# Splitting the early second products of a mixture-of-experts kernel, with their preparation shared between GpSimd and ScalarE

## The reference, cut to what matters

```python
for e in range(E):                                   # 8 experts
    h = jax.nn.gelu(x_flat @ w1[e].T + b1[e], approximate=False)   # 128 -> 512
    y = h @ w2[e].T + b2[e]                                        # 512 -> 128
    out = out + comb[:, e:e + 1] * y
```

## Time and profile before

| | us |
|---|---|
| median of 3 runs (lowest, highest) | 190.15 (190.08, 190.45) |
| the profiled execution, device time | 190.0 |
| its span, first to last instruction | 188.1 |
| TensorE busy in the span | 176.1 (94%) |
| ScalarE, VectorE, GpSimd busy | 123.4, 117.9, 79.0 |

### The profile page before, as it was taken

How to read it: one execution, slowest core, us unless ns; L and a number is a source line. 1 busy time by engine, 2 the same in 40 slices (tenths; PEclk the granted TensorE clock), 3 DMA queues, 4 the chain that set the end, 5 groups by cost and what they waited for, 6 DMA issues and landing times.

```text
span 188.1 us, 3342 instructions
## 1 busy us (share of the span) xinstructions
PE 176.1 (94%) x1281; PEld 120.3 (64%) x1281; DVE 117.9 (63%) x199; ACT 123.4 (66%) x185; POOL 79.0 (42%) x68
## 2 busy tenths in 40 slices
PE   6999999879899998999989999799999999999991
PEld 3269767456467543447556557467787888878880
DVE  1569434858184388556065919878789686676673
ACT  3525834225737654344989498848878999999980
POOL 8304219973922084552436073505221243333312
PEclk9999999999999999999999999999999999999999
DMA  4997000000000000490000000000000590000001
GB/s 136 316 384 324 7 0 0 3 0 0 3 3 2 2 0 0 110 331 12 0 0 5 0 0 0 0 3 0 0 7 3 186 302 14 0 3 0 0 0 56
DMA packets 5647, 10.41 MB, mean 55 GB/s; under 512 B 1264, under 2 KB 1648, under 8 KB 5376
## 3 DMA queue, kind: packets, MB, share of 16 engines
q1 hardware_dynamic: 5216, 10.12, 15.5%
q10 hardware_dynamic: 416, 0.08, 0.2%
HBM read 9.65 MB, written 0.56 MB: 54 GB/s over the span
## 4 chain that ended last, share of the span: by engine, by line
PE 73%; issue 9%; DVE 7%; ACT 5%; POOL 4%; DVEq 0%; ACTq 0%; POOLq 0%
PE PS L1157 8%; PE PS L1161 7%; PE PS L1158 6%; PE PS L1187 6%; PE PS L1184 6%; PE PS L1185 5%; PE PS L1179 4%; POOL pairs L353 4%; PE PS L851 3%; PE PS L1029 2%; PE PS L1015 2%; PE PS L906 2%; PE PS L874 2%; PE PS L1102 2%; ACT room L513 2%
## 5 line engine op out<-in xcount | busy, mean ns | idle before, releaser
L513 ACT ACTIVATE room<-PS,b_sb 128x512 f32<-128x512 f32 x64 | 43.6, 688 | 23.9 <-PE PS L1161 22.5
L768 DVE TENSOR_TENSOR Gl<-room,Gh 128x512 fp32r<-128x512 f32 x50 | 41.2, 832 | 13.6 <-ACT Gh L458 13.0
L361 POOL TENSOR_TENSOR x_sb<-x_sb,room 128x512 f32<-128x512 f32 x15 | 23.5, 1566 | 57.6 <-DVE room L777 57.6
L1157 PE MATMUL PS<-x2h,w1h 128*128 128x512 f32 x64 | 27.4, 427 | 1.1 <-ACT room L513 0.6
L458 ACT ACTIVATE Gh<-room 128x512 fp32r<-128x512 f32 x40 | 25.3, 633 | 1.3
L1161 PE MATMUL PS<-x2l,w1h 128*128 128x512 f32 x64 | 25.5, 399 | 0.0
L1158 PE MATMUL PS<-x2h,w1l 128*128 128x512 f32 x64 | 25.2, 393 | 0.0
L1184 PE MATMUL PS<-Gh,w2h 128*128 128x512 f32 x50 | 20.9, 418 | 0.0
L1187 PE MATMUL PS<-Gl,w2h 128*128 128x512 f32 x50 | 19.8, 397 | 1.0 <-DVE Gl L768 1.0
L1185 PE MATMUL PS<-Gh,w2l 128*128 128x512 f32 x50 | 19.7, 395 | 0.0
L1157 PEld LDWEIGHTS PS<-x2h,w1h 128*128 128x128 f32 x64 | 12.0, 187 | 10.4 <-issue 4.9
(11 more groups left out here) (136 smaller groups left out, 292.6 us busy)
## 6 DMA issues: line engine op xcount, KB each, us to landing
room<-comb_rows SPq DMA_DIRECT2D x16, 256.0 KB, 6.0
w1raw<-w SPq DMA_DIRECT2D x8, 256.0 KB, 5.0
w_sb<-w SPq DMA_DIRECT2D x2, 1024.0 KB, 9.6
x_sb<-x SPq DMA_DIRECT2D x2, 256.0 KB, 3.2
out<-x_sb SPq DMA_DIRECT2D x2, 256.0 KB, 4.4
attw_sb<-attw SPq DMA_DIRECT2D x1, 320.0 KB, 5.4
cst<-consts SPq DMA_DIRECT2D x1, 228.5 KB, 5.1
convw_sb<-convw ACTq DMA_DIRECT2D x1, 80.0 KB, 3.2
```

Source lines behind the costliest of these rows:

```text
L361: nc.gpsimd.tensor_tensor(t2[:, cols(p)], t2[:, cols(p)], part[:, s, :], ALU.add).then_inc(acc_done, 1)
L513: nc.scalar.activation(G[:, n % GR, :], PS[:, U_BANK[n % 2], :], ACT.Gelu, bias=b1_sb[:, c:c + 1])\
L768: nc.vector.tensor_tensor(Gl[:, n % GR, :], G[:, n % GR, :], Gh[:, n % GR, :].bitcast(f32), ALU.subtract)\
L1157: mm(o, w1h[e][:, ms], x2h[:, cols(p)], start=True, stop=False)
```

## The change

All second products are split but those of steps 18 and 22 (before, steps 0 to 11, 17 and 18 were unsplit). For steps 0 to 11 ScalarE makes the casts, and GpSimd the differences of steps 0 to 9. In steps 0 to 10 second products lag by three steps (before, by one for steps 0 to 8). The w2 of experts 0 to 2 is cast ahead of the loop, behind the exponentials of the first images, and the others in steps 2 to 6. GpSimd's w2 differences are made ahead of rstd(3) for expert 0, and in steps 1, 3, 8, 10, 12, 17, 21 for the others.

```diff
-W2_ORDER = [3, 4, 5, 6, 7, 0, 1, 2]
+EARLY_W2 = 3
-        LAGS = [1] * 9 + [2, 3, 4, 2, 3, 4] + [5, 2, 3, 4] * 2 + [5, 2] + [3] * (MT * VISITS - 25)
+        LAGS = [3] * 11 + [4, 2, 3, 4] + [5, 2, 3, 4] * 2 + [5, 2] + [3] * (MT * VISITS - 25)
...
-        SPLIT0, ACT_HIGH = 3 * MT, 24
-        SPLIT = [n for n in range(SPLIT0, STEPS) if n not in (17, 18)]
-        HIGH_W2 = {n: e for n, e in enumerate(W2_ORDER)}
-        LOW_W2 = {n + 1: e for n, e in enumerate(W2_ORDER)}
+        DVE_HIGH = range(3 * MT, 24)
+        SPLIT = [n for n in range(STEPS) if n not in (18, 22)]
+        HIGH_W2 = {e - 1: e for e in range(EARLY_W2, E)}
+        LOW_W2 = {1: 1, 3: 2, 8: 3, 10: 4, 12: 5, 17: 6, 21: 7}
+        POOL_LOW = range(10)
+
+        def low_engine(n):
+            return "pool" if n in POOL_LOW else "dve"
...
+            def low_gelu(n):
+
+                pool.wait_ge(g_high[high_engine(n)], high_count(n))
+                nc.gpsimd.tensor_tensor(Gl[:, n % GR, :], G[:, n % GR, :], Gh[:, n % GR, :].bitcast(f32), ALU.subtract)\
+                    .then_inc(g_low["pool"], 1)
...
+            low_weights2(0)
             rstd(3)
             rstd(4)
...
                 if n in SCORES:
                     for s in range(2):
                         pair(SCORES[n], s)
+                if n in POOL_LOW:
+                    low_gelu(n)
                 if n in LOW_W2:
                     low_weights2(LOW_W2[n])
...
                 k = n - GR
                 if k in SPLIT:
-                    act.wait_ge(g_low, split_count(k))
+                    act.wait_ge(g_low[low_engine(k)], low_count(k))
...
+            for e in range(EARLY_W2):
+                high_weights2(e)
             norm_square(3)
...
-                if n >= ACT_HIGH:
+                if n in SPLIT and high_engine(n) == "act":
                     high_gelu(n)
...
-                if n in SPLIT and n < ACT_HIGH:
+                if n in SPLIT and high_engine(n) == "dve":
                     high_gelu(n)
-                if n in SPLIT:
+                if n in SPLIT and low_engine(n) == "dve":
                     low_gelu(n)
...
-                pe.wait_ge(g_low, split_count(n))
+                pe.wait_ge(g_low[low_engine(n)], low_count(n))
```

More of the change, by code:

```diff
@@ L181, in hybrid_program @@
         g_high = {name: sem(f"g_high_{name}") for name in ("act", "dve")}
-        g_low = sem("g_low")
+        g_low = {name: sem(f"g_low_{name}") for name in ("pool", "dve")}
         up_done, gelu_done, down_done = sem("up_done"), sem("gelu_done"), sem("down_done")
@@ L229, in hybrid_program, with low_count @@
         G_LOGITS, G_ORDER, G_EXP, G_WEIGHTS, G_ROWS = 0, 1, 2, 2, 4
-        SPLIT0, ACT_HIGH = 3 * MT, 24
-        SPLIT = [n for n in range(SPLIT0, STEPS) if n not in (17, 18)]
-        HIGH_W2 = {n: e for n, e in enumerate(W2_ORDER)}
-        LOW_W2 = {n + 1: e for n, e in enumerate(W2_ORDER)}
+        DVE_HIGH = range(3 * MT, 24)
[5 more added lines that the diff above has]
+            return "pool" if n in POOL_LOW else "dve"
+        def low_count(n):
+            return sum(low_engine(k) == low_engine(n) for k in SPLIT if k <= n)
         def high_engine(n):
-            return "dve" if n < ACT_HIGH else "act"
+            return "dve" if n in DVE_HIGH else "act"
         def high_count(n):
             return sum(high_engine(k) == high_engine(n) for k in SPLIT if k <= n)
-        def split_count(n):
-            return sum(k <= n for k in SPLIT)
         def downs(n):
@@ L338, in low_weights2 @@
             def low_weights2(e):
-                pool.wait_ge(w2h_ready, W2_ORDER.index(e) + 1)
-                if e == W2_ORDER[0]:
+                pool.wait_ge(w2h_ready, e + 1)
+                if e == 0:
                     pool.wait_ge(pv_done, 4)
@@ L456, in high_gelu @@
                 act.wait_ge(gelu_done, n + 1)
-                act.wait_ge(down_done, n - GR + 1)
+                if n == 0:
+                    act.wait_ge(pv_done, 4)
+                    act.wait_ge(sums_done, 4)
+                if n >= GR:
+                    act.wait_ge(down_done, n - GR + 1)
                 nc.scalar.activation(Gh[:, n % GR, :], G[:, n % GR, :], ACT.Copy)\
@@ L757, in high_gelu @@
                 dve.wait_ge(gelu_done, n + 1)
[L758 to L762, removed]
+                dve.wait_ge(down_done, n - GR + 1)
                 nc.vector.tensor_copy(Gh[:, n % GR, :], G[:, n % GR, :]).then_inc(g_high["dve"], 1)
@@ L768, in low_gelu @@
                 nc.vector.tensor_tensor(Gl[:, n % GR, :], G[:, n % GR, :], Gh[:, n % GR, :].bitcast(f32), ALU.subtract)\
-                    .then_inc(g_low, 1)
+                    .then_inc(g_low["dve"], 1)
             def weigh(k):
@@ L1181, in down @@
                 if m == 0:
-                    pe.wait_ge(w2l_ready, W2_ORDER.index(e) + 1)
+                    pe.wait_ge(w2l_ready, e + 1)
                 pe.wait_ge(g_high[high_engine(n)], high_count(n))
```

## The result

The changed kernel takes 196.42 us (median of 4 runs, 196.17 to 196.60), the kernel before 190.12 beside it: a ratio of 1.033, 95% interval 1.031 to 1.035. The direction was forecast, the size was not: +6.3 us, where +1.8 was predicted and 193.5 was the upper end of the range.

The account below looks back on a forecast made before the run. TensorE was taken to bound overall, ScalarE in steps 10 to 13 and VectorE at steps 4 and 24. Terms 0.5 + 0.95 - 0.1 + 0.6 + 0.5 - 0.2 - 0.5 = +1.75 gave 191.9 us, range 189.7 to 193.5.

Parts of the forecast that it names:

- Steps 0 to 4: First loop steps: small gating operations on VectorE held by GpSimd's differences, raw scores of step 4 later, +0.95 us.
- the port: In top_weights, two small VectorE operations (line 746 and comb) each wait 1.24 us for GpSimd's differences; +0.95 us together.
- Rival (1): In top_weights, GpSimd takes a third turn ahead of line 743: 1.24 us more, 193.1 us; chance 0.24.
- Ahead of the loop: Before step 0: GpSimd's first w2 difference delays VectorE's last attend addition, +0.5 us; ScalarE's three w2 casts cost nothing.
- Steps 4 to 10: Split products save 0.16 us each, down(6) adds 0.70 in step 9: net -0.1, of which +0.06 behind raw(5).
- Steps 10 to 14: ScalarE's casts of gelu(10) and gelu(11) delay up(13) by +0.6 us and up(14) by +0.5 us.
- Steps 15 to 24: Step 16 saves 0.2 us; unsplit 22 in step 24 gains 0.5, against added VectorE and GpSimd work.
- best case: At step 24, unsplit product 22 ends at 119.8 us in place of 121.0: at best -1.2 us.
- walk: Work of steps 15 to 24 followed in order: VectorE and GpSimd delays lose nearly all the gain, giving -0.1 us.
- The 0.2 of step 16: Splitting the second product of 11, done in step 16 where TensorE runs through, saves 0.2 us.
- (4): Casts and GpSimd's row as forecast, but step 24's walk or the cover of scores(4) fails: 193.2 to 194; chance 0.06.
- Behind step 25: After the loop's first 25 steps the order of work is the same, so only its start can differ.

Follow-up runs that it names:

- order-only experiment: Changed kernel with GpSimd's gate_exp of the first half put ahead of the gelu difference of step 1 and w2 difference of expert 1: 193.28 us, ratio 1.011.
- the kernel kept busy: Changed kernel with 20 TensorE passes whose results nobody reads, ahead of the raw scores of step 4: 195.05 us, ratio 1.022.
- the kernels with the port free: Changed kernel with gate_exp first and GpSimd waiting for the gating weights before step 1's gelu difference, 189.32 us; also kernels built on it.
- the kernel with VectorE's casts: Changed kernel with the gelu casts of steps 10 and 11 made by VectorE, not ScalarE: 198.12 us, ratio 1.037.

## Why the prediction was right in direction and wrong in size

The prediction said 191.9 and 189.7 to 193.5; measured was 196.4. Its sum was +1.75, the spans differ by 6.7. The missing 4.9 are two items: the step that had gate_exp run ahead of the new differences (2.7), and a price for the clock that the sum did not have (2.2).

**Steps 0 to 4, the place of gate_exp: wrong.** The prediction wrote "Its inputs are there at 68.32 (gate_exp, 67.31 for 1.01)", and listed Gl(1) and w2l(1) behind it. In the code gate_exp is issued in step 2 of GpSimd's loop, and the two differences belong to step 1, so they come first. The trace of before couldn't show this by its order alone: there too gate_exp followed step 1's difference, but that was one, and it ended at 67.22, as the input came (67.24). Reading the numbers of the steps in place of the times would have told it. Cost: 2.8 us by the order-only experiment.

**The same step, the port: right.** Two operations were forecast as held behind g_sum and two were, line 762 slipped through as it was allowed to, and the maximum followed. With gate_exp first, raw(4) came at 74.06 where 73.9 was forecast. Rival (1), a third wait, didn't come in the changed kernel. The Trainium skill's rule (SBUF — State Buffer, Who interferes with whom) agrees with the pairs shown here: 1.00 for 0.42, 1.04 and 1.19 for 0.17, and for casts too, 1.50 for 0.42. The first held operation, g_sum (1.23), is a tensor_scalar with one SBUF input, which the prediction's wording of the rule leaves out; that section of the Trainium skill lists tensor_scalar too. What the rule leaves open is who follows when both wait: here a held VectorE operation got its turn between two of GpSimd's, and a dependent one behind it waited for a whole one again.

**The clock: missing.** The prediction counted TensorE's idle time as lost and the work behind it at full clock ("from raw to raw 2.24"). With 5.14 us idle the clock fell to its lower level, and step 4 took 2.15 us more, which the kernel kept busy got back. Even the prediction's own case would have had 1.6 of it, so 191.9 should have been 193.5 on its own reading. Before, the longest wait of TensorE that the chain of waits showed in the loop was 0.96 us, so no row there priced it; but the prediction itself forecast a hole of 2 us or more ahead of raw(4), longer than any it had rows for, and put the clock's part at nothing without a reason.

**Ahead of the loop: right**, +0.57 for +0.5, shown by moving the difference. ScalarE's three casts were hidden (its idle time ahead of the square went from 3.50 to 1.95).

**Steps 4 to 10: right**, +0.06 for +0.06. From raw to raw it is 2.24, the split product saves its 0.16, and down(6) costs its 0.7.

**Steps 10 to 14: right**, +0.51 and +0.45 for +0.6 and +0.5, shown by the kernels without these casts.

**Steps 15 to 24: near in sum.** The stretch to the sums of step 24 is -0.64 for -0.5. The -0.5 was a choice between a best case and a walk, so that it came out is in part luck: the best case of -1.2 is -1.33 where GpSimd has no w2 differences there, and the walk that said -0.1 was too dark (counted from the sums of step 16 and put on the times of before, weigh(3) came at 116.45 and not 116.9, and the pairs of step 23 ended at 121.6 and not 122.3). The 0.2 of step 16 didn't come: there the stretch was 0.06 longer, with up(14) to the first second product 0.1 longer and Gl(14) held by GpSimd's pairs (1.67). That this ate the saving was not tried by itself.

One sum of the rivals is off: (4) gives 193.2 to 194, but its two terms make 191.9 + 0.6 + 0.7 = 193.2, and 193.4 with the +0.3 at which the step 24 term ends. It does not touch the forecast.

**Behind step 25, nothing forecast: right**, 66.89 and 66.92.

## What to carry to other kernels

Before work is given to an idle in-order engine, list what it already issues, in the order of the code, and who waits for the smallest of these; here a 1.0 us exponential of four columns behind two new 1.27 us differences cost 2.8. GpSimd's free time isn't free for VectorE: in a dependent row of five small operations, three each waited 1.04 to 1.23 us for a GpSimd instruction; one wait on GpSimd kept it off the row and won 2.4 to 2.9 us. When a change opens a hole on TensorE like these (2.2 to 5.1 us), count the slow stretch behind it as well, or close the hole. And measure the parts of a change one by one: here one of them, which step is left unsplit, was worth 1.3 us on the old kernel by itself.

## What the runs showed of the hardware

The clock fell to 0.50 with stands of TensorE of 5.14, 2.37 and 2.24 us, and the lowered clock cost 2.15, 1.6 and 1.6 us. With the long stand it fell near 74.6, while TensorE still stood; with the two others it fell 0.2 and 0.5 us behind the end of the stand. Each of the three also had a wait of 0.9 us at raw(3), 2.3 us ahead of the stand; with that wait alone (the kernels with the port free) the clock stayed full. In the kernel with 22 split, two waits of 0.92 and 0.95 were followed by a slow stretch as well (2.72 grew to 4.22), but in the kernel with VectorE's casts two waits of 0.72 and 0.95, just as close together, were not (1.00 in every window of 1 us from 94 to 136). The prediction had no term for the clock.

A reciprocal on VectorE (one SBUF input, four columns) was not held by GpSimd in any of the six traces where it ran beside a difference: 0.18 at 73.13 in the changed kernel, while the addition behind it was held for 1.04 by the same difference. The sum for the gating, which has one SBUF input of four columns too, was held in all six (1.09 to 1.26).
